# Attention and fp4 feed-forward block: the gate and up weights loaded and prepared later, and the bias of q carried by a 129th column

## The reference

```python
xn = layernorm(x)
q, k, v = xn @ Wq + bq, ctx @ Wq + bq, ctx @ Wq + bq         # 256 -> 16
corr = real(ifft(fft(q) * conj(fft(k)))).mean(batch, channel)  # one row of 128 lags
w, lags = top_k(corr, 12); w = softmax(w)
R = sum(w_j * roll(v, -lag_j)); x = x + tile(R, 16 heads) @ Wout + bout
g, u = fp4(layernorm(x)) @ fp4(w_gate).T, fp4(layernorm(x)) @ fp4(w_up).T   # 256 -> 704
x = x + fp4(silu(g) * u) @ fp4(w_down).T                      # 704 -> 256
```

## Time and profile before

| | us |
|---|---|
| median of three runs (lowest, highest) | 572.26 (572.17, 574.67) |
| the profiled execution, its span | 570.98, 569.2 |
| TensorE, VectorE busy over the span | 466.8, 463.4 |
| ScalarE, GpSimd busy | 394.4, 284.1 |
| first stage ends (start of line 523) | 90.56 |
| long stage's first matmul | 130.66 |

### The profile page before, as it was taken

One profiled execution on the slowest core, in us unless ns is written; L12 is line 12 of the kernel. 1 busy time (PEld: TensorE's weight loads), 2 busy tenths in 40 slices (PEclk: granted clock), 3 DMA queues, 4 the chain that ended last, 5 costly groups with the idle time before them and its releaser, 6 DMA issues. The chain is left out here.

```text
span 569.2 us, 10045 instructions
## 1 busy us (share of the span) xinstructions
PE 466.8 (82%) x3454; PEld 307.0 (54%) x3454; DVE 463.4 (81%) x748; ACT 394.4 (69%) x666; POOL 284.1 (50%) x366
## 2 busy tenths in 40 slices
PE   5277995408799899998989999998999999999944
PEld 5266994303355555655556555565555655556633
DVE  2899657356889999989999999998999999997760
ACT  2378555456887778888887777888888777776530
POOL 3053530066556665565566666555556666622231
PEclk9699998757899999999999999999999999999977
DMA  9965930323246665555655576555655556445433
GB/s 276 306 220 157 293 119 15 87 57 76 51 84 119 128 118 113 107 123 120 124 117 106 126 117 129 108 109 129 120 117 116 112 126 109 95 89 107 79 78 78
DMA packets 165042, 69.19 MB, mean 122 GB/s; under 512 B 129152, under 2 KB 164736, under 8 KB 164992
## 3 DMA queue, kind: packets, MB, share of 16 engines
q1 hardware_dynamic: 164416, 68.03, 52.9%
q10 hardware_dynamic: 576, 0.53, 0.3%
HBM read 27.90 MB, written 9.18 MB: 65 GB/s over the span
## 5 line engine op out<-in xcount | busy, mean ns | idle before, releaser
L723 PE MATMUL ps<-guT_hi,a_xT 128*128 128x512 f16 (+1 forms) x384 | 140.6, 366 | 50.3 <-DMA a_xT<-ctx_sb 50.3
L428 POOL TENSOR_TENSOR ctx_sb<-h_c,sl 128x704 f16<-128x704 f16 x64 | 96.1, 1523 | 115.8 <-DVE ctx_sb L953 115.8
L733 PE MATMUL ps<-dT_hi,hqT 128*128 128x256 f16 x704 | 132.5, 277 | 11.9 <-DMA hqT<-ctx_sb 11.9
L724 PE MATMUL ps<-guT_lo,a_xT 128*128 128x512 f16 (+1 forms) x384 | 140.3, 365 | 0.0
L725 PE MATMUL ps<-guT_hi,a_xT 128*128 128x512 f16 (+1 forms) x384 | 140.0, 365 | 0.0
L723 PEld LDWEIGHTS ps<-guT_hi,a_xT 128*128 128x128 f16 x384 | 37.8, 98 | 98.6 <-DMA a_xT<-ctx_sb 40.4
L735 PE MATMUL ps<-dT_lo,hqT 128*128 128x256 f16 x384 | 89.6, 277 | 0.0
L482 ACT ACTIVATE h_c<-y_h 128x1408 bf16<-128x1408 bf16 (+3 forms) x40 | 49.2, 1230 | 55.2 <-DVE y_h L983 35.0
L733 PEld LDWEIGHTS ps<-dT_hi,hqT 128*128 128x128 f16 x704 | 70.0, 99 | 25.0 <-DMA hqT<-ctx_sb 12.7
L466 POOL TENSOR_TENSOR xs<-xs,w_raw 128x512 f32<-128x512 f32 x32 | 38.1, 1192 | 69.5 <-issue 49.1
L948 DVE SCALAR_TENSOR_TENSOR hb<-ps,h_in,w_raw 128x704 f32<-128x704 f32 x64 | 60.5, 945 | 2.6 <-PE ps L725 2.5
(11 more groups left out here) (140 smaller groups left out, 854.9 us busy)
## 6 DMA issues: line engine op xcount, KB each, us to landing
w_raw<-a_scratch SPq DMA_DIRECT2D x64, 128.5 KB, 2.7
xs<-in_x_dram SPq DMA_DIRECT2D x16, 512.0 KB, 5.7
ctx_sb<-in_ctx_dram SPq DMA_DIRECT2D x16, 512.0 KB, 4.5
out_dram<-a_xT SPq DMA_DIRECT2D x64, 128.0 KB, 2.0
hqT<-ctx_sb SPq DMA_TRANSPOSE x64, 3.7
w_raw<-in_L_ffn_w_down_dram SPq DMA_DIRECT2D x1, 704.0 KB, 5.2
w_raw<-in_L_ffn_w_gate_dram SPq DMA_DIRECT2D x1, 640.0 KB, 5.9
w_raw<-in_L_ffn_w_up_dram SPq DMA_DIRECT2D x1, 640.0 KB, 7.1
```

The costliest lines, as they stand in the source:

```text
L428: pool.tensor_tensor(hq[:, j % 2, t, FF:2 * FF].rearrange("p (ih r) -> p ih r", ih=IH), h_c[:, :].bitcast(F16).rearrange("p (ih t r) -> p ...
L723: pe.matmul(dst, xt[:, c, :], guT[0][:, c, n0:n1], start=(c == 0), stop=False)
L724: pe.matmul(dst, xt[:, c, :], guT[1][:, c, n0:n1], start=False, stop=False)
L733: pe.matmul(dst, hqT[:, j % 4, c, :], dT_hi[:, c, :], start=(c == 0), stop=False)
```

## The change

Three things. The four loads of the gate and up weights are issued behind the loads of the groups 0 to 3 instead of behind groups 0 and 1. Their preparation starts later and is spread: `w_prepare(0)` in turn 2, `largest(0)` on GpSimd in turn 2 behind `rstd_a(4)`, the segments in the turns 3, 5, 7, 9, 11 and 13, with `w_finish` one turn and `w_hi` and `w_lo` two turns behind. And the second matmul of each group (k by the bias) is gone: q has a 129th column, which holds the bias, so one matmul with 129 columns gives both; the column of the sum is added when the matrix is copied out, by one more copy on ScalarE and a bias in the two copies that were there.

```diff
+W_FIRST = 3
-        qkT = sb("qkT", [P, 2, 2, P])
+        qT = sb("qT", [P, 2, P + 1])
+        kT = sb("kT", [P, 2, P])
+        g_bias = sb("g_bias", [P, 1])
+        def turn(i):
+            k = i - W_FIRST
+            return k // 2 if k >= 0 and k % 2 == 0 and k // 2 < N_GU else None
 # SyncE
-            for m, w in enumerate((w_gate, w_up)):
...
             for i in range(2, NQ):
+                if i == AHEAD:
+                    half, whole = FF - FF // P * P, FF // P
+                    for m, w in enumerate((w_gate, w_up)):
...
                 load_x(i)
                 load_c(i)
 # GpSimd
             rstd_a(0)
             rstd_a(1)
-            largest(0)
             for i in range(NQ):
                 if i + 2 < NQ:
                     rstd_a(i + 2)
-                if 0 <= i - 2 < N_GU:
-                    w_lo(i - 2)
+                if i == W_FIRST - 1:
+                    largest(0)
+                if turn(i - 2) is not None:
+                    w_lo(turn(i - 2))
 # ScalarE
-                if 0 <= i < N_GU:
-                    w_split(i)
-                if 0 <= i - 2 < N_GU:
-                    w_hi(i - 2)
+                if turn(i) is not None:
+                    w_split(turn(i))
+                if turn(i - 2) is not None:
+                    w_hi(turn(i - 2))
             act.wait_ge(s["g_done"], NQ)
-            act.activation(g2[:, 0, :], bank(7)[:, 0:P], ACT.Copy).then_inc(s["g_ev"], 1)
-            act.activation(g2[:, 1, :], bank(7)[:, 0:P], ACT.Copy).then_inc(s["g_ev"], 1)
+            act.activation(g_bias[:, :], bank(7)[:, P:P + 1], ACT.Copy).then_inc(s["g_col"], 1)
+            act.wait_ge(s["g_col"], 1)
+            for k in range(2):
+                act.activation(g2[:, k, :], bank(7)[:, 0:P], ACT.Identity, bias=g_bias[:, 0:1]).then_inc(s["g_ev"], 1)
 # TensorE
-                pe.matmul(bank(7)[:, 0:P], qkT[:, i % 2, 1, :], qkT[:, i % 2, 0, :], start=(i == 0), stop=False)
-                pe.matmul(bank(7)[:, 0:P], qkT[:, i % 2, 1, :], bq_col[:, :].broadcast_to([P, P]), start=False, stop=(i == NQ - 1)
+                pe.matmul(bank(7)[:, 0:P + 1], kT[:, i % 2, :], qT[:, i % 2, :], start=(i == 0), stop=(i == NQ - 1)
                           ).then_inc(s["g_done"], 1)
 # VectorE
-            w_prepare(0)
+            for k in range(2):
+                last = dve.tensor_copy(qT[:, k, P:P + 1], bq_col[:, :])
+            last.then_inc(s["q_bias"], 1)
             for i in range(NQ):
                 if i + 2 < NQ:
                     stats_a(i + 2)
                 if i >= 1:
                     evac_qk(i - 1)
-                if i == 0:
+                if i == W_FIRST - 1:
+                    w_prepare(0)
+                if i == W_FIRST:
                     w_scales(0)
-                if 0 <= i - 1 < N_GU:
-                    w_finish(i - 1)
-                if 0 <= i < N_GU:
-                    w_segment(i)
+                if turn(i - 1) is not None:
+                    w_finish(turn(i - 1))
+                if turn(i) is not None:
+                    w_segment(turn(i))
```

More of the change, by code:

```diff
@@ L196, in build @@
             "stats", "pool_a", "wq_sum", "r_ev", "wq_mid", "trx", "trc", "evx", "evc", "proj", "qk_ev", "v_tr", "v_ev",
-            "g_done", "g_ev", "g_io", "t_steps", "t_pe", "t_exp", "t_io", "a_io0", "a_io1", "a_io2", "a_io3", "m_sums",
+            "q_bias", "g_done", "g_col", "g_ev", "g_io", "t_steps", "t_pe", "t_exp", "t_io", "a_io0", "a_io1", "a_io2", "a_io3", "m_sums",
             "x1_done", "sq_done", "pool_st", "xn_ready", "x_max", "sc_steps", "sh_done", "s32", "sl", "x_split", "x4_steps",
@@ L307, in _ @@
             load_c(1)
-            half, whole = FF - FF // P * P, FF // P
-            for m, w in enumerate((w_gate, w_up)):
[L310 to L314, removed]
-            for i in range(2, NQ):
+            for i in range(2, NQ):
+                if i == AHEAD:
+                    half, whole = FF - FF // P * P, FF // P
+                    for m, w in enumerate((w_gate, w_up)):
+                        c0, r0 = m * (whole + 1), m * half
+                        sp.dma_start(w_raw[:, c0 * D:(c0 + whole) * D].rearrange("p (c n) -> p c n", n=D),
+                                     w[r0:r0 + whole * P].rearrange("(c p) n -> p c n", p=P)).then_inc(s["w_loaded"], 16)
+                        sp.dma_start(w_raw[m * half:m * half + half, whole * D:(whole + 1) * D], w[(1 - m) * whole * P:(1 - m) * whole * P + half]
+                                     ).then_inc(s["w_loaded"], 16)
                 load_x(i)
@@ L635, in correlate @@
                 pe.wait_ge(s["qk_ev"], i + 1)
-                pe.matmul(bank(7)[:, 0:P], qkT[:, i % 2, 1, :], qkT[:, i % 2, 0, :], start=(i == 0), stop=False)
-                pe.matmul(bank(7)[:, 0:P], qkT[:, i % 2, 1, :], bq_col[:, :].broadcast_to([P, P]), start=False, stop=(i == NQ - 1)
+                if i == 0:
+                    pe.wait_ge(s["q_bias"], 1)
+                pe.matmul(bank(7)[:, 0:P + 1], kT[:, i % 2, :], qT[:, i % 2, :], start=(i == 0), stop=(i == NQ - 1)
                           ).then_inc(s["g_done"], 1)
                 need(pe, s["v_ev"], i // QT)
-                pe.transpose(bank(6)[:, P * (i % QT):P * (i % QT + 1)], qkT[:, i % 2, 1, :], ident[:, :]).then_inc(s["v_tr"], 1)
+                pe.transpose(bank(6)[:, P * (i % QT):P * (i % QT + 1)], kT[:, i % 2, :], ident[:, :]).then_inc(s["v_tr"], 1)
             for i in range(NQ):
@@ L825, in evac_qk @@
                 out = bank(4 + i % 2)
-                dve.tensor_scalar(qkT[:, i % 2, 1, :], out[:, P:2 * P], bq_col[:, 0:1], None, ALU.add)
-                dve.tensor_copy(qkT[:, i % 2, 0, :], out[:, 2 * P:3 * P]).then_inc(s["r_ev"], 1)
+                dve.tensor_scalar(kT[:, i % 2, :], out[:, P:2 * P], bq_col[:, 0:1], None, ALU.add)
+                dve.tensor_copy(qT[:, i % 2, 0:P], out[:, 2 * P:3 * P]).then_inc(s["r_ev"], 1)
                 dve.wait_ge(s["r_ev"], i + 1)
-                dve.tensor_tensor(qkT[:, i % 2, 0, :], out[:, 0:P], qkT[:, i % 2, 0, :], ALU.mult).then_inc(s["qk_ev"], 1)
+                dve.tensor_tensor(qT[:, i % 2, 0:P], out[:, 0:P], qT[:, i % 2, 0:P], ALU.mult).then_inc(s["qk_ev"], 1)
             def w_prepare(part):
```

## The result

| | before | changed |
|---|---|---|
| median (lowest to highest), runs | 572.39 us (570.21 to 576.2), 18 | 575.71 us (573.96 to 578.91), 18 |
| ratio to before, 95% interval | | 1.0061 (1.0044 to 1.0078) |
| the profiled execution, its span | 570.98, 569.2 | 577.43, 575.6 |
| first stage ends | 90.56 | 94.27 |
| long stage's first matmul | 130.66 | 135.09 |

What follows compares the result with a forecast made beforehand. VectorE was taken to bound the first stage while weights are prepared, TensorE behind the last segment. Stage +0.6, column +0.2 and clock +1.7 gave +2.5 on 572.26, 574.8 us; range 568.8 to 578.2.

Steps and rivals of the forecast that it cites:

- Loads: First four turns: TensorE's early stop removed, x group 4 landing unchanged at 21.98, the weights' 4.06 us wait gone; nothing lasting.
- The maximum over the partitions: GpSimd, turn 2: 7.54 us load before the maximum, 8.70 until GpSimd is back; second segment ends at 46.3.
- The rival at 569.8: GpSimd's configuration costs little: maximum starts at 27.9 instead of 32.9, everything behind 5.0 us earlier, -2.5; chance 0.18.
- Segments in every second group: Turns 5 to 13: pairs of turns take 9.40 us with a wait for v, 7.92 without; reaching 80.6.
- The end of the stage: From turn 14: `evac_qk(14)` at 88.0, then last two steps of 1.75 and 1.44; line 523 starts at 91.2.
- The bias column: Removed matmul saves 0.23 us in each of the last two steps; column copy on ScalarE costs 0.2 (0.1 to 0.4).
- TensorE's clock: One fall at the wait for v in turn 6, costing 1.7 us; bounds 0 and three falls, 5.1.
- My rival: Clock falls at all three waits for v (turns 6, 10, 14), 1.7 us each: +5.9, 578.2; chance 0.24.
- The long stage: Sign: it should keep its length; the prediction is wrong if it changes by over a microsecond.
- Sum: Whole kernel: +0.6 for the stage, +0.2 column, +1.7 clock, together +2.5 us, 574.8.
- within 0.5%: Whole kernel indistinguishable from no change, between 569.4 and 575.1 us; chance 0.47, against 0.38 slower and 0.15 faster.

Runs made afterwards that it cites:

- max_rstd3: Changed kernel with the first maximum on GpSimd one place earlier, ahead of `rstd_a(4)` instead of behind it: 575.81 us, ratio to before 1.0069.
- every_turn: Changed kernel with the segments in consecutive turns, 3 to 8, instead of every second: 576.38 us, ratio to before 1.0067.
- column_only: Kernel before with only the 129th column; loads and segments stay as before: 572.19 us, ratio to before 0.9999.
- column_again: Kernel before with the 129th column alone, run once more for a second profile: 571.13 us, ratio to before 0.9990.
- max_tensor: Changed kernel with the first maximum over the partitions taken by TensorE and VectorE instead of GpSimd: 575.49 us, ratio to before 1.0046.
- v_early: Changed kernel with ScalarE taking v in turns 5, 9 and 13 instead of 6, 10 and 14: 569.11 us, ratio to before 0.9951.
- no_column: Changed kernel with the bias of q by its own matmul again and the matrix copied out as before: 575.07 us, ratio to before 1.0057.
- column_v_early: Kernel before with the 129th column and v taken in turns 5, 9 and 13: 569.96 us, ratio to before 0.9964.

## Why the prediction was right

Its steps give 92.9 for the stage's end (91.2 and one fall of 1.7); 94.27 was measured, of which 1.47 is x group 4, which landed at 23.45 instead of 21.98. From the landing on it is 70.92 predicted and 70.82 measured. That agreement is partly luck, as the steps show:

- *Loads.* The early stop of TensorE is halved; the prediction had it removed. TensorE finished its first four turns by 20.63, then stood for 5.46 us up to 26.09 (10.93 before) behind VectorE, which waited 6.45 us for x group 4. Its clock fell again during that stop, to 0.50 from 25 to 30 us; the sum has no term for this fall, and it needed none: VectorE, which leads here, was busy for 4.90 of these 5 us. The landing "at the same time" was wrong as well, by 1.47 us in this execution. It was later than 21.98 in all eight executions with the changed order, 22.24 to 23.45, on average by 0.8, so part of this probably belongs to the change; why was not tried.
- *The maximum over the partitions.* The mechanism is right, and max_rstd3 shows it. The sizes: 7.29 for 7.54, 7.99 for 8.70, `rstd_a(4)` 0.1 us earlier from the landing; `stats_a(7)` 43.66 for 43.2, the second segment's end 46.76 for 46.3, which is 1.0 less from the landing on. The Trainium skill's figure for such a load (GPSIMD Engine Reference, section 2.1 Instruction dispatch, 5.95 us) lies at the lower end of what the executions show where the maximum started later than its operand allowed: 5.97 us in every_turn to 8.08 in column_only, with 7.85 in column_again, where no releaser is shown. What was wrong is the price of "this step I price highest": everything behind the maximum would come 5.0 us earlier with a cheap configuration. It would have been 1.6 at most, since the first split, the evacuation and a group at the low clock stand just behind it (max_tensor, one execution). I had followed VectorE and GpSimd, and not TensorE through the turns 3 and 4, where the clock had fallen a second time. The rival at 569.8 is contradicted by max_tensor, which has no load at all and a median of 575.49.
- *Segments in every second group.* Predicted 9.40 with the fall's 1.7, 7.92, 9.40, 7.62 from one segment's end to the next; measured 11.05, 8.34, 9.43 and about 8.1. The path through ScalarE and `v_all` is the right one; v_early shows it. The waits at line 652 were not "some 4 us" each, but 4.47, 2.81 and 1.90. The pairs without it are 0.4 too short in my sum: in the first, 0.18 is a wait for `rstd_a`, the remainder small pieces of 0.03 to 0.12.
- *The end of the stage.* 1.75 and 1.46 for the last two steps, where I had 1.75 and 1.44.
- *The bias column.* "The two `g2` copies change function and keep their size" was wrong: with the column copy the store stands 0.38 us later, where I took 0.2, and the trip of the matrix 0.3 more in this execution. The 0.46 that I gave it in the stage is borne out (0.57 in no_column). By these pieces it is no gain in the changed order but a loss of about half a microsecond, below what a median can tell; the medians point both ways (575.07 without it against 575.71, 569.09 without it against 568.39).
- *TensorE's clock.* The prediction counted one fall in all. The changed kernel had three: during the stop up to 26.09, near 35 us, and at the first wait for v. Only the third lies on the path that the sum follows; the second slows the path that was at most 1.6 us shorter. Of the third: the pair was 11.0 to 12.0 us long (second segment to third) in all four versions that keep this wait and its order (changed, no_column, max_rstd3, max_tensor), so this fall is no accident. The second wait was 2.81 us in the changed kernel, in max_rstd3 and in max_tensor, and the clock fell in the last alone. My rival's condition, that the later waits be "about 4 us long", was therefore too strict.
- *The long stage.* The prediction called itself wrong if this stage changed by over a microsecond, and between the two profiled executions it changed by 1.97. The other twelve executions, 438.3 to 439.8 us, speak for scatter, so the sign was set too tight; nothing explains the 1.97.
- *Sum.* +2.5 predicted; +3.3 by the medians, +6.4 between the two profiled executions. The first difference is small against the pieces: the pairs (+0.9), the load (-1.0), the column's part of the chain (+0.5), and the landing (+1.47 in this execution, +0.8 on average). The number came out because these errors cancel in part.

What the prediction did not look for is that the wait behind `v_all`, which it priced only as part of the pairs, is worth more than the entire change: 6.6 us. Nor did it give its best chance to what happened: "within 0.5%" had 0.47, slower 0.38, and the median is above its limit of 575.1.

## What to carry to other kernels

When work is spread over more turns of a loop, look at what it now stands ahead of in each of these turns, on every queue. Here half as many segments at a time changed little; that three times instead of once a segment's split stood ahead of a copy for which TensorE waits cost all of it, and moving that copy by one turn turned a loss of 0.6% into a gain of 0.5%, of which the same move gives 0.3% without the change. A wait in the profile is worth only its distance to the next path: ahead of pricing its removal, follow the other engines through the same turns, with the clock that they will have.

## What was not expected of the hardware

- GpSimd needs 7.5 to 8.7 us from the start of the maximum to its next instruction, in every execution whose first maximum is on GpSimd (7.99 in the changed kernel). The maximum itself is over early: VectorE uses its result at 34.49, 0.03 us after its record ends. I read the rest as the way back from the maximum's library. An earlier configuration instruction did not shorten it (7.90 in max_rstd3). The load ahead of the maximum took 6.0 to 8.1 us where nothing else held the maximum back, and could be hidden (max_rstd3).
- TensorE's clock fell in or just behind a wait of 4.47 us, in or behind waits of 2.21 and 2.81 in max_tensor, not at 2.81 in the changed kernel, and near 36 us at 2.66 in column_again and 1.98 in column_v_early but not at 2.69 in the kernel before. The idle time ahead, as one trace shows it, does not tell it.
- From the store of the same matrix it took 1.71 to 1.73 us to the issue behind it in the five executions without the column, and 1.74 to 2.29 in the nine with it. This is unexplained.
- A VectorE instruction with two inputs waits for a GpSimd instruction that started first. Of the changed kernel, GpSimd and then VectorE:

```profile
61.43 1.17 POOL L402 TENSOR_TENSOR w_q_lo<-hb,w_q_hi 128x512 f16<-128x512 f32 x1
```

```profile
61.61 1.53 DVE L818 TENSOR_TENSOR hb<-h_c,w_s 128x512 f32<-128x512 f16 x1
```

Undisturbed the second takes 0.69 us (at 51.16). It is shown as busy, without a bracket, and ends 0.54 us after the first (62.60 and 63.14). The Trainium skill (SBUF — State Buffer, section SBUF: two separate sides) says that the port pair which the two engines share is held by one of them for a whole instruction, while the other is blocked; the trace agrees. The 2.36 us of a segment's finish in the earlier trace rows had such a wait in them, at another of its instructions, and so held: 2.37 here.
